# The same row numbers and own engine orders for pair 0, with the next tile's block loads issued between group 0's and group 1's row gathers

## The chip, the cores and the metric

One core of one Trainium2 chip. The metric is the device time of one execution in microseconds (us). The times of several runs are given as a median; one further execution was profiled, and all rows below come from it.

## What is computed

32 samples of 32 tokens with 256 channels run through four layers, each added to its input: windowed attention over a paged key/value cache, two mixing layers with weights picked per sample, and a gated feed-forward with low-rank adapters per sample. Cut to what matters:

```python
def reference(x, table, lens, cond, subj, side, ...):
    # attention: q, k, v from x; rms norm of q and k; rope; new k, v written into the cache
    # at positions lens + t; each query sees the 128 last positions up to its own
    x = x + attention(x, Wq, Wk, Wv, Wo, q_scale, k_scale, k_blocks, v_blocks, table, lens)
    x = x + einsum('bct,bcd->bdt', x, L1_weights[cond])
    x = x + einsum('bct,bcd->bdt', x, L2_weights[subj]) + side[subj][:, :, None]
    gate = lora_linear(x, Wg, Ag, Bg, subj)
    up = lora_linear(x, Wu, Au, Bu, subj)
    return x + lora_linear(silu(gate) * up, Wd, Ad, Bd, subj)
```

The cache lies in blocks of 16 positions; `table` names 257 blocks per sample, of which 11 can matter for a query window.

## The kernel before, in words

The kernel is written by hand, engine by engine: each engine has a fixed list of instructions, and semaphores join them.

**Units of work.** The 32 samples form 8 groups of 4 (128 tokens, one row of the partitions each), and two groups form a pair. Attention and the mixing layers go by group, the feed-forward by pair (256 tokens as the moving side of the products). The old cache is read by tiles of 8 samples, so tile t serves pair t.

**Cache rows.** For each tile GpSimd loads the blocks (`load_blocks`, L623 to L628: one indirect DMA for k, one for v, both into the buffer `early`), and SyncE stores them from `early` as rows of 256 values into a table in device memory (`scatter_rows`, L534 to L543, eight stores). The new k and v of all samples, held in `new_kv`, are stored behind them (`new_rows`, L545). Then GpSimd gathers for each group the 160 rows per sample that its queries see (`prepare`, L640 to L656: four indirect DMAs `far` and one `near`). Their row numbers (`rows`, then `place_i`) are computed on VectorE and TensorE (L991 to L1004). `prepare` of a group waits for the tile's stores, for the new rows and, from group 2 on, for the P.V products of the group two before it, whose buffer it takes. `load_blocks` of a tile waits for the stores of the tile before, since there is one `early`.

**Prologue.** Projections of v and k, then q (L1217), the rope products on VectorE, squares and roots for the norms on ScalarE (`root`, L732), turning q (L1240) and spreading its scales.

**Attention of a group**, in stages: "kt" transposes the gathered keys, "scores" multiplies, adds the mask and takes the row maxima on VectorE (L1069) and the exponentials on ScalarE (L778), "den" takes the reciprocals on VectorE (L1081) and scales the probabilities on GpSimd (`normalise`, L658 to L669), "pt0" and "pt1" transpose them, "pv" multiplies by v, "wo" projects and adds to x, "mix" applies the composed mixer, "xt" and "xf" turn the result and split it into a high and a low part for the feed-forward.

**Mixer.** The two mixing layers are composed on the chip into one matrix per sample: block matrices `first_bd` and `second_bd` are transposed ("first", L1312) and multiplied ("prod", L1320) in two halves of four groups. The buffers of these two are taken by Wd afterwards (`d_raw`), so SyncE waits for the second product (L587, semaphore `mixer_psum`) before it loads Wd.

**Feed-forward of a pair.** Each operand is split in a high and a low part and each product is three matmuls (L1427): "lora", "adapt", "gate0" to "up7", "down..", "tail..". Pair 0 has attention alone; during the feed-forward of pair m the attention of pair m + 1 is interleaved. The weights are split once, step by step, during pair 0 and the first feed-forward ("high" on ScalarE, "low" on VectorE, "split" both, L799 and L1168; TensorE waits for a split with "use").

**What sets the order.** `START_ORDER` (pair 0), `FIRST_ORDER` (feed-forward 0 with attention of pair 1) and `LOOP_ORDER` are lists of steps; every engine walks the same list and takes its part of each step. GpSimd takes only "den", "gather" and "load".

**SyncE's queue** is one list: inputs, tile 0's stores, new rows, mixer rows, adapter weights a, g0, mixer blocks, b0, u0, tile 1's stores, b1, g1, u1, then behind the wait for the mixer Wd (L589), eight loads of Ad (L594), Bd (L596), and the stores of tiles 2 and 3.

## Time and profile before

| | us |
|---|---|
| median of 3 runs | 257.56 (257.46 to 262.0) |
| profiled execution, its own time | 257.65 |
| its span | 255.2 |
| TensorE busy | 209.8 (82%) |
| VectorE busy | 142.6 (56%) |
| ScalarE busy | 105.2 (41%) |
| GpSimd busy | 76.8 (30%) |

The span is what lies between the first and the last instruction that the profiler saw; the execution's own time is 2.45 us more. TensorE's busy time is the longest, but it has idle stretches in the first half: the slices of the page show it full only from about 130 us on. PE is TensorE, DVE VectorE, ACT ScalarE, POOL GpSimd, SP SyncE; a q behind a name is its queue of DMA issues.

### The profile page before, as it was taken

To read this page: it belongs to the slowest core of one execution; us is meant where nothing else is said; L and a number is where in the kernel's file an instruction comes from. 1 tells how busy PE (TensorE), PEld (TensorE's weight loads), DVE (VectorE), ACT (ScalarE), POOL (GpSimd) and SP (SyncE) were. 2 spreads that over 40 slices of the span, in tenths; PEclk is the share of its full clock that TensorE was granted. 3 is DMA by queue.
4 is the path that set the end of the run, shared out by engine and by line. 5 is a ranking of instruction groups with operands and counts; after the bars stand their busy time and mean duration, and the time that the engine had idled before them with its cause. 6 is when DMAs were issued, how large, how long until landed. Compare 5 with 4: busy or idle time off the path is not lost.

```text
span 255.2 us, 5101 instructions
## 1 busy us (share of the span) xinstructions
PE 209.8 (82%) x1995; PEld 190.1 (75%) x1995; DVE 142.6 (56%) x486; ACT 105.2 (41%) x290; POOL 76.8 (30%) x90
## 2 busy tenths in 40 slices
PE   2696968478768649892999799999979999989995
PEld 1675858367456638882988799888878988889995
DVE  5745979575457545696514754741665454236522
ACT  2146228595532652557012733452282364213310
POOL 3520047543677040048242325045240013000000
PEclk9999999956999977998599999999999999999999
DMA  6988799669942988815795003001300000010001
GB/s 167 264 167 111 188 180 326 180 124 136 240 161 91 249 143 111 132 49 134 160 144 145 5 0 105 0 3 46 100 0 4 0 3 0 3 41 3 0 0 44
DMA packets 64124, 25.25 MB, mean 99 GB/s; under 512 B 55780, under 2 KB 60836, under 8 KB 63524
## 3 DMA queue, kind: packets, MB, share of 16 engines
q1 hardware_dynamic: 60432, 14.07, 27.5%
q0 software_dynamic: 2944, 10.23, 15.5%
q10 hardware_dynamic: 724, 0.62, 0.8%
q8 instruction: 16, 0.26, 0.5%
q14 instruction: 8, 0.07, 0.1%
HBM read 17.83 MB, written 7.08 MB: 98 GB/s over the span
## 4 chain that ended last, share of the span: by engine, by line
PE 44%; DVE 14%; issue 12%; POOL 11%; SPq 7%; ACT 6%; DMA 5%; POOLq 1%; ACTq 0%; DVEq 0%
PE bank L1427 27%; PE bank L1217 6%; POOL far L651 5%; SPq L594 4%; POOL prob L665 4%; DMA early<-in_kb,blk_i 3%; SPq L540 3%; ACT prob L778 2%; DVE prob L1069 2%; PE bank L1374 2%; PE bank L1413 2%; DVE mask L1048 1%; PE bank L1393 1%; PE bank L1206 1%; DVE low_raw L1115 1%
## 5 line engine op out<-in xcount | busy, mean ns | idle before, releaser
L651 POOL DMA_INDIRECT far<-table_rows,place_i x32 | 31.7, 991 | 63.2 <-issue 26.4
L1427 PE MATMUL bank<-xf_high,gu_high 128*128 128x256 f32 x128 | 39.0, 305 | 0.2 <-DVE b_low L1168 0.2
L778 ACT ACTIVATE prob<-prob,ntop,qscale 128x160 f32<-128x160 f32 x64 | 32.4, 508 | 15.9 <-DVE ntop L1075 15.9
L1427 PE MATMUL bank<-xf_high,gu_low 128*128 128x256 f32 x128 | 36.4, 284 | 0.0
L1427 PE MATMUL bank<-xf_low,gu_high 128*128 128x256 f32 x128 | 36.4, 284 | 0.0
L665 POOL TENSOR_TENSOR prob<-prob,rden 128x512 f32<-128x512 f32 x16 | 17.1, 1066 | 61.6 <-DVE rden L1081 61.5
L1105 DVE SCALAR_TENSOR_TENSOR gs<-th,bank 128x256 f32<-128x256 f32 x32 | 13.4, 419 | 26.5 <-ACT th L813 26.1
L1427 PEld LDWEIGHTS bank<-xf_high,gu_high 128*128 128x128 f32 x128 | 24.5, 192 | 1.7 <-issue 1.0
L1374 PE MATMUL bank<-k,prob 128*128 128x128 f32 x64 | 13.1, 340 | 14.7 <-POOL prob L665 14.7
L1427 PEld LDWEIGHTS bank<-xf_low,gu_high 128*128 128x128 f32 x128 | 24.5, 191 | 0.2
L1427 PEld LDWEIGHTS bank<-xf_high,gu_low 128*128 128x128 f32 x128 | 24.4, 191 | 0.0
L813 ACT ACTIVATE th<-bank 128x256 f32<-128x256 f32 x32 | 11.9, 379 | 27.8 <-PE bank L1427 27.8
L1374 PEld LDWEIGHTS bank<-k,prob 128*128 128x128 f32 x64 | 8.9, 171 | 17.5 <-POOL prob L665 17.4
L1427 PE MATMUL bank<-d_high,h_high 128*128 128x256 f32 x64 | 20.6, 322 | 0.0
L1069 DVE CUSTOM_DVE_ANT_0 prob<-bank,mask 128x160 f32<-128x160 f32 x64 | 17.0, 320 | 4.8 <-PE bank L1366 4.8
L1427 PE MATMUL bank<-low_high,b_high 128*128 128x256 f32 x64 | 18.7, 292 | 0.2
L1427 PE MATMUL bank<-d_low,h_high 128*128 128x256 f32 x64 | 18.7, 292 | 0.0
L1427 PE MATMUL bank<-d_high,h_low 128*128 128x256 f32 x64 | 18.5, 289 | 0.0
L1427 PE MATMUL bank<-low_low,b_high 128*128 128x256 f32 x64 | 18.2, 284 | 0.0
L1427 PE MATMUL bank<-low_high,b_low 128*128 128x256 f32 x64 | 18.2, 284 | 0.0
L1098 DVE TENSOR_TENSOR h_low<-hf,h_high 128x256 fp32r<-128x256 f32 x32 | 16.1, 504 | 0.1
L1366 PE MATMUL bank<-k_t,q_bd 64*128 64x160 f32 x128 | 12.0, 331 | 3.4 <-ACT k_t L772 1.3
(220 smaller groups left out, 527.3 us busy)
## 6 DMA issues: line engine op xcount, KB each, us to landing
table_rows<-early SPq DMA_DIRECT2D x32, 144.0 KB
table_rows<-far_probs SPq DMA_DIRECT2D x2, 512.0 KB, 3.9
gu_raw<-in_Wg SPq DMA_DIRECT2D x2, 512.0 KB, 5.5
gu_raw<-in_Wu SPq DMA_DIRECT2D x2, 512.0 KB, 6.0
d_raw<-in_Wd SPq DMA_DIRECT2D x2, 512.0 KB, 8.9
out<-xs SPq DMA_DIRECT2D x8, 128.0 KB, 1.8
xs<-in_x ACTq DMA_DIRECT2D x1, 512.0 KB, 4.9
xs<-in_x SPq DMA_DIRECT2D x1, 512.0 KB, 5.8
```

Of the source, the lines that this page charges most:

```text
L594: sp.dma_start(ad_raw[:, k * NR:(k + 1) * NR].rearrange("p (n r) -> p n r", r=RANK), Ad[:, k * P:(k + 1) * P, :].rearrange("n p r -> p n r ...
L651: pool.indirect_dma_start(far[r][:, s, :], None, seen, bass.IndirectOffsetOnAxis(ap=far_i[:, GB * n + s:GB * n + s + 1], axis=0)).then_inc ...
L665: pool.tensor_tensor(v, v, over(scale, 2, P), ALU.mult).then_inc(prob_ready, 1)
L778: last = act.activation(v, v, ACT.Exp, bias=ntop[r][:, j:j + 1], scale=qscale[:, n, j:j + 1], accum_out=den[r][:, j:j + 1])
L813: act.activation(th[f % 3][:, :], FFN_BANKS[f % 3][:, 0:PAIR_TOK], ACT.Tanh, scale=0.5).then_inc(tanh_ready, 1)
L1069: last = dve.tensor_tensor_reduce(prob[twin(n)][:, j // 2, j % 2, :], b[(2, 0)[half] + j % 2][:, s * SPAN:(s + 1) * SPAN], mask[twin(n)][: ...
L1098: dve.tensor_tensor(h_low[:, f, :], hf[f % 2][:, :], h_high[:, f, :].bitcast(F32), ALU.subtract).then_inc(h_ready, 1)
L1105: dve.scalar_tensor_tensor(gs[f % 2][:, :], th[f % 3][:, :], 1.0, b[:, 0:PAIR_TOK], ALU.add, ALU.mult).then_inc(gs_ready, 1)
L1217: last = pe.matmul(bank[dst][:, t * D:(t + 1) * D], x_t[:, k, 2 * i + t, :], w_vkq[:, k, cols], start=(k == 0), stop=(k == KD - 1))
L1366: last = pe.matmul(b[(2, 0)[half] + c][:, s * SPAN:(s + 1) * SPAN], q_bd[q, n, 2 * half + s, :, :, :].rearrange("p c h t -> p (c h t)"), k ...
L1374: last = pe.transpose(b[2 + half][:, j * P:(j + 1) * P], prob[twin(n)][:, 2 * half + j // 2, j % 2, 0:P], ident)
L1427: last = pe.matmul(dst, w[a], x[b], start=start and n == 0, stop=stop and n == 2)
```

## The change

It gives each engine a list of its own for pair 0, moves parts of the prologue, and moves one pair of block loads.

- **Row numbers**: on VectorE their computation stands before the rope products of k, on TensorE their sums stand before the second projection of v and k and their transposes before the projections of q. The broadcasts of `subj` and of the norm scales go to bank 6. The addition to the mixer's diagonal stands behind `place_i`.
- **ScalarE**: the table for the square root is loaded ahead by a primer, the first root stands before the last squares of k, w_o is copied last; on TensorE w_o's transposes stand last.
- **SyncE**: Wo is loaded behind the new rows; b1 is loaded before tile 1's stores.
- **GpSimd**: `prepare(0)`, `load_blocks(1)`, `prepare(1)`. For pair 0 it no longer scales probabilities.
- **Pair 0**: `START_PE`, `START_ACT`, `START_DVE`, `START_POOL`. New stages "exp0" and "exp1" (exponentials of one half) on ScalarE, "norm0" and "norm1" (reciprocals and scaling of one half) on VectorE.
- **First feed-forward**: "kt" of group 2 before "up0", the second half of the mixer ("first", 1 and "prod", 1) behind the scores of group 2, b1's split behind "gate0", the mask of group 2 already in pair 0. The wait for the mixer moves from the scores to the transposes.

```diff
+START_PE = [("kt", 0), ("scores", 0), ("first", 0), ("kt", 1), ("pt0", 0), ("scores", 1), ("pt1", 0), ("prod", 0),
+            ("pv", 0), ("wo", 0), ("mix", 0), ("pt0", 1), ("xt", 0), ("pt1", 1), ("pv", 1), ("wo", 1), ("mix", 1), ("xt", 1)]
...
+START_POOL = [("gather", 0), ("gather", 1), ("load", 2)]
 FIRST_ORDER = (
-    [("use", "a"), "lora", "adapt", ("low", "b1"), ("mask", 0), ("use", "g0"), "gate0", ("first", 1), ("use", "u0"), ("use", "b1"),
-     "up0",
-     ("kt", 0), ("prod", 1), ("scores", 0), ("mask", 1), "gate1", "up1", ("den", 0), "gate2",
...
+    [("use", "a"), "lora", "adapt", ("use", "g0"), "gate0", ("low", "b1"), ("use", "u0"), ("use", "b1"), ("kt", 0), "up0",
+     ("scores", 0), ("mask", 1), "gate1", ("first", 1), "up1", ("den", 0), ("prod", 1), "gate2", "up2",
...
@@ SyncE
-            for a in range(2):
-                for h in range(GS):
-                    sp.dma_start(wo_raw[:, a, h, :].rearrange("p (g d) -> p g d", g=G),
...
             new_rows(0)
             new_rows(1)
+            for a in range(2):
+                for h in range(GS):
+                    sp.dma_start(wo_raw[:, a, h, :].rearrange("p (g d) -> p g d", g=G),
...
                 if a == 0:
                     gate_up("u0", Wu, 1, lower)
-                    scatter_rows(1)
+            scatter_rows(1)
@@ GpSimd
-            for r in R:
-                prepare(r, r)
+            prepare(0, 0)
             load_blocks(1)
+            prepare(1, 1)
@@ ScalarE
+            act.activation(primer[:, 1:2], ones[:, 0:1], ACT.Sqrt)
             for i in range(4):
                 take_vk(i)
-            root(1, 0, KHALF * G)
+                if i == 2:
+                    root(1, 0, KHALF * G)
@@ VectorE
+                elif stage in ("norm0", "norm1"):
+                    half = int(stage[4])
+                    dve.wait_ge(exp_ready, 2 * n + half + 1)
+                    q = slice(4 * half, 4 * half + 4)
+                    dve.reciprocal(rden[r][:, q], den[r][:, q]).then_inc(rden_ready, 1)
...
+                    dve.tensor_tensor(v, v, over(rden[r][:, q], 2, P), ALU.mult).then_inc(prob_ready, 1)
...
@@ TensorE
                 else:
-                    pe.wait_ge(x1_ready, 1)
+                    pe.wait_ge(top_ready, 6)
```

GpSimd, from the side gather of the prologue to the first work on pair 1, before. `early` is the block buffer, `far` and `near` are a group's gathered rows, `prob` its probabilities:

```order
L637 DMA side_b<-in_side,subj_i 32x32
L651 DMA far<-table_rows,place_i 128x256 x4
L654 DMA near<-table_rows,place_i 128x256
L651 DMA far<-table_rows,place_i 128x256 x4
L654 DMA near<-table_rows,place_i 128x256
L627 DMA early<-in_kb,blk_i 72x2048
L627 DMA early<-in_vb,blk_i 72x2048
```

and in the changed kernel, with the semaphores that each waits for:

```order
L643 DMA side_b<-in_side,subj_i 32x32
L657 DMA far<-table_rows,place_i 128x256 [waits v_out0,new_out,k_out0,place_ready]
L657 DMA far<-table_rows,place_i 128x256 x3
L660 DMA near<-table_rows,place_i 128x256
L633 DMA early<-in_kb,blk_i 72x2048 [waits k_out0]
L633 DMA early<-in_vb,blk_i 72x2048 [waits v_out0]
L657 DMA far<-table_rows,place_i 128x256 [waits v_out0,new_out,k_out0,place_ready]
L657 DMA far<-table_rows,place_i 128x256 x3
L660 DMA near<-table_rows,place_i 128x256
```

The two loads into `early` have moved ahead of the five gathers of group 1.

ScalarE in pair 0, from the key copy of group 0, before. `a_high` and `gu_high` are weight splits, `mixer` is the copy of the first mixer product, `prob` rows are the exponentials, half a group each two rows:

```order
L772 COPY k_t<-bank 128x4x128 [waits kt_psum]
L778 ACTIVATE prob,den<-prob,ntop,qscale 128x160 [waits ntop_ready]
L778 ACTIVATE prob,den<-prob,ntop,qscale 128x160 x3
L778 ACTIVATE prob,den<-prob,ntop,qscale 128x160 [waits ntop_ready]
L778 ACTIVATE prob,den<-prob,ntop,qscale 128x160 x3
L799 CAST a_high<-a_raw 128x512 [waits w_in_a]
L799 CAST gu_high<-gu_raw 128x2x512 [waits w_in_g0]
L778 ACTIVATE prob,den<-prob,ntop,qscale 128x160 [waits ntop_ready]
L778 ACTIVATE prob,den<-prob,ntop,qscale 128x160 x3
L778 ACTIVATE prob,den<-prob,ntop,qscale 128x160 [waits ntop_ready]
L778 ACTIVATE prob,den<-prob,ntop,qscale 128x160 x3
L783 COPY far_probs<-bank 128x512 [waits pfar_psum]
```

and now, from group 0's second half of exponentials:

```order
L786 ACTIVATE prob,den<-prob,ntop,qscale 128x160 [waits ntop_ready]
L786 ACTIVATE prob,den<-prob,ntop,qscale 128x160 x3
L791 COPY far_probs<-bank 128x512 [waits pfar_psum]
L807 CAST a_high<-a_raw 128x512 [waits w_in_a]
L840 COPY mixer<-bank 128x512 [waits mixer_psum]
L786 ACTIVATE prob,den<-prob,ntop,qscale 128x160 [waits ntop_ready]
L786 ACTIVATE prob,den<-prob,ntop,qscale 128x160 x3
L794 COPY o_t<-bank 128x4x2x32 [waits o_psum]
L786 ACTIVATE prob,den<-prob,ntop,qscale 128x160 [waits ntop_ready]
L786 ACTIVATE prob,den<-prob,ntop,qscale 128x160 x3
```

The copies of the transposed probabilities of group 0 and of the mixer product now stand ahead of the exponentials of group 1.

TensorE in the first feed-forward, from "up0"'s last product, before. `first_bd` rows are the transposes of the mixer's second half, `second_bd` rows its product, `far` and `near` the keys and `k_t` the scores of group 2:

```order
L1427 MATMUL bank<-low_high,b_low 128x256
L1345 MATMUL bank<-k,far 128x128 [waits firstt_ready,o_ready,xf_ready,x1_ready,kv_in0]
L1345 MATMUL bank<-k,far 128x128 x3
L1346 MATMUL bank<-k,near 128x128
L1320 MATMUL bank<-second_bd,first_t 128x128 [waits x3_ready,firstt_ready]
L1320 MATMUL bank<-second_bd,first_t 128x128 x3
L1366 MATMUL bank<-k_t,q_bd 128x160 [waits mixer_ready,x3_ready,xf_ready,near_kt_ready,far_kt_ready]
L1366 MATMUL bank<-k_t,q_bd 128x160 x7
```

and now, from the scores of group 2 ("up0" stands before them, the first three products are "gate1", the nine behind the transposes, of which five rows are shown, "up1"):

```order
L1381 MATMUL bank<-k_t,q_bd 128x160 [waits x3_ready,xf_ready,near_kt_ready,far_kt_ready]
L1381 MATMUL bank<-k_t,q_bd 128x160 x7
L1444 MATMUL bank<-low_high,b_high 128x256
L1444 MATMUL bank<-low_low,b_high 128x256
L1444 MATMUL bank<-low_high,b_low 128x256
L1333 MATMUL bank<-k,first_bd 128x128 [waits top_ready]
L1333 MATMUL bank<-k,first_bd 128x128 x3
...
L1444 MATMUL bank<-low_high,b_high 128x256
L1444 MATMUL bank<-low_low,b_high 128x256
L1444 MATMUL bank<-low_high,b_low 128x256
L1339 MATMUL bank<-second_bd,first_t 128x128 [waits firstt_ready]
L1339 MATMUL bank<-second_bd,first_t 128x128 x3
```

The product of the second half stood before the scores of group 2 and now stands behind them, "gate1" and "up1", and its transposes wait for the row maxima (`top_ready`).

## Rows read from the trace of the kernel before

**Rows 1.** The chain that ended last, 82 to 125 us: start, duration, what.

```profile
82.58 0.37 SPq L589
...
84.51 4.35 SPq L594
...
94.42 15.74 issue
...
110.93 0.99 POOL far L651
...
120.18 1.07 POOL prob L665
...
121.29 1.12 PE bank L1374 x4
```

**Rows 2.** Timeline of SyncE's queue: start, duration from first to last issue, what.

```profile
82.58 0.92 SPq L589 DMA_DIRECT2D d_raw<-in_Wd  x2
83.54 13.64 SPq L594 DMA_DIRECT2D ad_raw<-in_Ad  x8
...
97.92 35.40 SPq L540 DMA_DIRECT2D table_rows<-early  x16
```

**Rows 3.** Timeline of GpSimd, first and last gather of pair 0 and the loads.

```profile
34.52 0.97 POOL L651 DMA_INDIRECT far<-table_rows,place_i  x1 [20.09 <-DVE place_i L1004]
...
45.80 0.95 POOL L654 DMA_INDIRECT near<-table_rows,place_i  x1 [0.30 <-issue]
47.05 0.97 POOL L627 DMA_INDIRECT early<-in_kb,blk_i  x1 [0.30 <-issue]
```

**Rows 4.** Store of new rows (L550, the later took 3.1) and side gather (L637), with landing.

```profile
L550 SPq DMA_DIRECT2D table_rows<-far_probs x2: 359/666/972, 26.5 to 30.1; - x2
...
DMA to landing us min/median/max: 3.1/3.9/4.7
...
L637 POOL DMA_INDIRECT side_b<-in_side,subj_i x1: 877/877/877, 13.6 to 13.6; - x1
...
DMA to landing us min/median/max: 6.9/6.9/6.9
```

**Rows 5.** The v block loads of tile 1 and tile 2 (L627), with landing.

```profile
L627 POOL DMA_INDIRECT early<-in_vb,blk_i x1: 969/969/969, 48.3 to 48.3; - x1
...
DMA to landing us min/median/max: 8.8/8.8/8.8
...
L627 POOL DMA_INDIRECT early<-in_vb,blk_i x1: 964/964/964, 82.6 to 82.6; - x1
...
DMA to landing us min/median/max: 11.1/11.1/11.1
```

**Rows 6.** Windows: stretch, length, busy per engine, PEclk, DMA share, GB/s.

```profile
39.40:44.40 5.00, 4.10 (x43) 3.82 (x42) 4.49 (x15) 4.15 (x8) 3.79 (x4) 1.00 1.08 319
47.00:50.70 3.70, 1.36 (x16) 1.12 (x16) 2.42 (x19) 1.38 (x6) 1.94 (x2) 1.00 0.66 158
86.00:90.00 4.00, 1.83 (x16) 1.62 (x14) 2.00 (x11) 4.00 (x18) 0.00 (x0) 1.00 1.09 290
```

**Rows 7.** Timeline of TensorE: keys and scores of group 1, products, transposes of group 2.

```profile
50.78 0.66 PE L1345 MATMUL bank<-k,far 128*128 128x128 f32 x4 [2.18 <-DMA near<-table_rows,place_i]
...
52.78 2.50 PE L1366 MATMUL bank<-k_t,q_bd 64*128 64x160 f32 x16 [1.23 <-DVE k_t L1057]
...
73.84 0.36 PE L1427 MATMUL bank<-xf_high,a_high 128*128 128x256 f32 x1 [1.01 <-DVE xf_low L1093]
...
78.97 0.36 PE L1427 MATMUL bank<-xf_high,gu_high 128*128 128x256 f32 x1 [0.16 <-DVE b_low L1168]
...
92.58 1.12 PE L1374 MATMUL bank<-k,prob 128*128 128x128 f32 x4 [4.76 <-POOL prob L665]
```

**Rows 8.** Timeline of VectorE: a two-input product of 512 elements, a mask.

```profile
29.33 0.69 DVE L977 TENSOR_TENSOR far_probs<-k_sin,rstd 128x512 f32<-128x512 f32 x1
...
50.61 1.26 DVE L1048 SCALAR_TENSOR_TENSOR mask<-k,thresh 128x160 f32<-128x160 f32 x4
```

124 lines of the change are left out of this document (66 added, 58 removed), and 1 row of the table FIRST_ORDER.

## The prediction

> **What bounds the kernel now.** I read the chain that ended last first. Up to 73 us it runs through the attention of pair 0. Between 82.6 and 121.3 us it is no engine at all: it leaves TensorE for SyncE's queue [rows 1]. The loads of Wd (L589) start at 82.58, when the second half of the mixer has been composed on TensorE. Behind them stand eight loads of Ad (L594), of which the second holds the queue 4.35 us and the third about as long, and only then the sixteen stores of two cache tiles. GpSimd's gather of group 4 waits for the first eight until 110.93. GpSimd's order is fixed: behind that gather come the next block loads, and the softmax scaling of group 3 only at 120.18. TensorE has been done with its second down piece since 116.66 and starts the transposes of group 3 at 121.29, 4.63 us idle.
>
> SyncE's timeline gives the three points of this path [rows 2]: Wd at 82.58, the stores of tile 2 at 97.92 (15.3 us later), the gather 13.0 us after that. From there to 121.29 are 10.4 us of GpSimd. Then the kernel is mostly products to the end. So what happens before 80 us counts only through one number: when the Wd loads may start. That is what I work out.
>
> **Part 1, the prologue.** The row numbers are made on VectorE before the k path instead of behind it: some 2.5 us of small operations, which now fill the time in which VectorE waited 2.8 us for the square root. Moving ScalarE's table load (1.28 us) ahead removes that wait. k of the second half is then ready at 29.5 instead of 30.0, and the row numbers at once behind it, 4.4 us earlier than 34.25. But the gather also waits for the store of the new rows, issued 30.1 and landing 3.1 us later, 33.2 [rows 4]. It is the next to be late: the first gather goes at 33.1 instead of 34.52 [rows 3], a gain of 1.4 us. The rotation of q on VectorE starts when the last q projection is done, 32.8 instead of 34.8; w_o's transposes now sit before the key transposes of group 0, and these come at 43.8 instead of 45.25. Group 0 gains 1.4 us.
>
> **Part 2, the block loads between the gathers.** Five gathers of group 0 take 5 x 1.255 = 6.3 us, so the loads of tile 1 go at 39.4 and 40.7 instead of 47.05 and 48.33 [rows 3], and the five gathers of group 1 from 41.95, the last at 46.95 instead of 45.80. In the old kernel that last one landed at 50.7 and TensorE took the keys of group 1 at 50.78 [rows 7]. What do the loads in front of them cost? The nearest row: at the start of the program a gather of 4 KB (L637) issued behind a pair of such loads at 13.56 took 6.9 us, until 20.5, after the second load had landed (19.1) [rows 4]. So a gather behind a load lands behind it. Lower bound: no such order, 46.95 + 3.0 = 49.9. The second load takes 8.8 us with little beside it, 40.7 + 8.8 = 49.5, and 11.1 us beside other traffic, 51.8 [rows 5]; behind it 5 x 128 KB, about 3 us at some 200 GB/s (the windows of rows 6 have 158 to 319). That is 52.5 to 55, upper bound 56. The transfers now meet the weight loads: the 16 engines are full from 33.2 to 44.4 already (share 1.08 in its second half) and at 0.66 after 47 [rows 6]; to that come Wo (0.25 MB) and the first part of Bu (0.5 MB). I take 53.7 us for the keys of group 1, 2.9 later than before.
>
> The Trainium skill, "DMA: Bandwidth & Descriptors", section "Queues, rings and completion order", says that each DMA engine consumes the descriptors of one ring in order, which speaks against this move. The row of the 4 KB gather agrees. Without that rule the keys would be there at 49.9 and the total 3.8 us less than the sum below.
>
> **Part 3, the own orders for pair 0.** TensorE places the keys of group 1 ahead of the first transposes of group 0's probabilities, ready since 52.0; so group 0 waits too. Then: group 1's scores at the lower clock 2.50 us [rows 7], transposes 1.4, mixer product 1.9. ScalarE now stands with the mixer copy in front of group 1's exponentials, so these begin at about 61, where they began at 55.65. Against it: the scaling on VectorE takes about 0.7 us per half (the nearest row is L977, two inputs of the same shape, 0.69 [rows 8]) against 1.04 on GpSimd, and it does not wait behind two weight splits. Walking the four queues piece by piece from the keys of group 1 to the first feed-forward product I get 22.5 us: keys and copies 2.2, scores 2.5, transposes and mixer product 3.3, copy and four exponentials 2.7, o_t, Wo and x1 2.0, two scalings with the mask of group 2 between them (1.26 in [rows 8]) 3.5, transposes, their copies, P.V, Wo, mixing and split 6.3. Before it was 73.84 - 50.78 = 23.1. So the feed-forward of pair 0 begins at 53.7 + 22.5 = 76.2 instead of 73.84.
>
> **Part 4, the second half of the mixer.** Before, its product ended 8.7 us after the first feed-forward product. Now it stands behind "up0", the scores of group 2, "gate1" and "up1", and its transposes wait for all maxima of group 2. From the start S of the feed-forward: the split b1 ends at S + 5.1 (78.97 - 73.84 [rows 7], unchanged), keys 0.7, up0 1.1, tanh and two VectorE operations 1.3, so maxima from S + 8.2, 2.4 us, to S + 10.6; transposes 0.5, up1 1.1 (the copy of the transposes with the mask before it, 1.2 + 0.7, ends at S + 12.5), product 1.0 and rounding: S + 13.7. Wd goes at 89.9 instead of 82.58: +7.3 us.
>
> **Part 5, what SyncE's queue gives back.** In the old kernel the loads of tile 2 (issued 81.3 and 82.6, the later one landing at 93.65) run beside Wd, and the DMA engines are full (1.09 from 86 to 90 [rows 5, 6]). Now GpSimd gathers pair 1 from about 63 (the first P.V of pair 0 releases it; tile 1's stores are done at about 61 instead of 67.7) and from about 72, and issues those loads at 78; they are down at 87. Wd is then alone: 0.5 MB loads issued back to back at 65.1 and 65.6 landed after 5.5 and 6.3 us, so the third Ad load gives the queue free at +6.5 instead of +11.1, and the stores follow at +10.8 instead of +15.3. Saving 4.5 us; bounds 0 and 7.5 (every issue at its shortest).
>
> **The sum.** Stores of tile 2: 89.9 + 10.8 = 100.7 against 97.92, +2.8 us. Stores, gather, block loads and scaling from there on keep their 23.4 us (97.92 to 121.29 [rows 1, 2]). TensorE does not take the bound back: it reaches these transposes at S + 40.7 = 116.9, counting that its 4.76 us of idle at 92.58 [rows 7] shrinks to 1.5, and waits for GpSimd until 124.1. The profiled execution was 257.65 us (span 255.2 and 2.45 around it), the median 257.56: 257.65 + 2.8 = 260.4. Bounds: keys of group 1 at 49.9 (-3.8) or 56 (+2.3); the queue's saving 7.5 (-3) or 0 (+4.5).
>
> **Rivals.**
> A, the queue is not late: the gathers of group 1 are not held, pair 0 runs partly at the full clock, and the faster drain wins. 257.65 + 2.8 - 3.8 - 1 = 255.7. For it: SyncE's queue clearly suffers from the block loads now. Against: the 4 KB gather.
> B, slower by more than 2%: TensorE stays at its lower clock. In the old kernel it fell to 1.2 GHz after the idle stretch around 50 us (kt to scores of group 1: 2.50 us for what takes 1.36 at 47.25) and came back at 62 [rows 7]. In the new one it idles some 4 us before group 1's keys and is busy only half of 62 to 76. If it goes into the feed-forward at 1.2 GHz, lora and gate0 (30 products at 0.12 us a start) cost 3 us more, and pair 0 one to two, all ahead of Wd: 260.4 + 4.5 = 264.9. It decides once the extra delay is over 2.4 us. Against: gaps of the same kind at 63 to 73 left the clock up.
> C, faster by more than 2%: GpSimd's wait goes altogether and TensorE is the bound. It reaches the transposes at S + 40.7; with S = 72 that is 112.7 against 121.3, 249 us. It needs Wd before 79 us, against Part 4.
> D, the moves hide: everything before 80 us is swallowed and Wd is as late as the queue is shorter, 257.5.
>
> **How the numbers follow.** Forecast (259 to 262.5) 0.48, A 0.18, B 0.17, D 0.14, C 0.03. The range 255 to 265 takes in A, D and most of B. 2% is 5.15 us, about what a measurement of this kernel tells from no change: faster by more 0.03, within 0.79, slower by more (over 262.8: B and the upper edge of the forecast) 0.18.
>
> **What would show it.** First gather near 33.1; block loads of tile 1 at 39.4; group 1's keys on TensorE at 52 to 55; first feed-forward product 74.5 to 78; Wd's loads 88 to 92 with the mixer product as releaser; no Ad load holding the queue for 4 us twice; tile 2's stores near 100.7; TensorE idle 6 us or more before the transposes of group 3. It is wrong if Wd starts before 86 us, if the gathers of group 1 land before 51, or if that idle time on TensorE is gone.

## The result, and the profile after

The changed kernel takes 267.54 us (median of 4 executions, 265.05 to 269.31); the kernel before, on the same chip and beside it, 258.93 (257.46 to 262.0). The ratio is 1.0359, with a 95% interval of 1.0298 to 1.042: slower by 3.6%. The profiled execution took 266.96 us, its span 265.1. The ratios and their intervals leave out executions over 1.5% above the fastest of the same kernel (1 of 4 here, 6 of 11 in f3, 5 of 10 in f2, 2 of 4 in f4, 4 of 6 in g1) while the medians take all, so a ratio can differ from the quotient of two medians.

The page of the changed kernel, TensorE's slices with the granted clock and the DMA share under them, and the chain's shares:

```profile
PE   2798886048577978893199979999998999989995
...
PEclk9999999856965879999579999999999999999999
DMA  6787999999723609791578601200400000010001
...
PE 41%; issue 12%; DVE 12%; POOL 8%; ACT 6%; DMA 4%; SPq 1%; POOLq 0%
```

A slice is 6.6 us. TensorE has a slice with nothing (46 to 53 us), and a slice of 1 at 126 to 133 us. The DMA engines are full from 27 to 66 us. "issue", 12% of the chain, is for the most part GpSimd's wait for the stores of a cache tile, in which the profile shows nothing to wait for.

GpSimd's timeline (start, duration, what, idle time before it): first and last gather of group 0, the two block loads, first and last gather of group 1, first gather of group 4, scaling of group 3. It answers to [rows 3] and to the end of [rows 1].

```profile
33.30 0.97 POOL L657 DMA_INDIRECT far<-table_rows,place_i  x1 [18.93 <-DMA table_rows<-far_probs]
...
38.34 0.95 POOL L660 DMA_INDIRECT near<-table_rows,place_i  x1 [0.30 <-issue]
39.59 0.97 POOL L633 DMA_INDIRECT early<-in_kb,blk_i  x1 [0.31 <-issue]
...
47.23 0.95 POOL L660 DMA_INDIRECT near<-table_rows,place_i  x1 [0.31 <-issue]
...
121.66 0.99 POOL L657 DMA_INDIRECT far<-table_rows,place_i  x1 [19.72 <-issue]
...
130.57 1.05 POOL L671 TENSOR_TENSOR prob<-prob,rden 128x512 f32<-128x512 f32 x1
```

TensorE's timeline: keys of group 0, first half of the mixer's blocks, keys and scores of group 1, the Wo product of group 1, the first feed-forward products, the mixer's second product, the transposes of group 3 [rows 7].

```profile
43.84 0.66 PE L1362 MATMUL bank<-k,far 128*128 128x128 f32 x4 [0.58 <-DMA near<-table_rows,place_i]
...
54.23 1.11 PE L1333 MATMUL bank<-k,first_bd 128*128 128x128 f32 x4 [7.60 <-DMA second_bd<-mix_rows]
57.69 1.12 PE L1362 MATMUL bank<-k,far 128*128 128x128 f32 x4 [2.33 <-DMA near<-table_rows,place_i]
...
60.04 2.50 PE L1381 MATMUL bank<-k_t,q_bd 64*128 64x160 f32 x16 [0.17 <-issue]
...
76.18 2.08 PE L1424 MATMUL bank<-w_o,o_t 128*128 128x256 f32 x4 [0.61 <-ACT o_t L794]
...
82.26 0.55 PE L1444 MATMUL bank<-xf_high,a_high 128*128 128x256 f32 x1 [1.01 <-DVE xf_low L1114]
...
96.42 1.91 PE L1339 MATMUL bank<-second_bd,first_t 128*128 128x128 f32 x8
...
131.68 1.11 PE L1391 MATMUL bank<-k,prob 128*128 128x128 f32 x4 [9.68 <-POOL prob L671]
```

SyncE's queue: the mixer's blocks, Bu, the stores of tile 1, and from Wd to the stores of tile 2 [rows 2].

```profile
39.76 2.07 SPq L559 DMA_DIRECT2D second_bd<-mix_rows  x4
...
43.46 0.99 SPq L587 DMA_DIRECT2D b_raw<-in_Bu  x1
48.85 15.32 SPq L541 DMA_DIRECT2D table_rows<-early  x8
...
98.36 0.92 SPq L595 DMA_DIRECT2D d_raw<-in_Wd  x2
99.32 8.37 SPq L600 DMA_DIRECT2D ad_raw<-in_Ad  x8
...
108.43 38.18 SPq L541 DMA_DIRECT2D table_rows<-early  x16
```

Read against the rows of before, the distance grows in three steps. The keys of group 1 come at 57.69 instead of 50.78: +6.9. From them to the first feed-forward product S it is 24.6 us instead of 23.1, and from S to the end of the mixer's second product, right behind which Wd is loaded, 16.1 instead of 8.7: +7.4. Then SyncE's queue gives back 5.3: Wd to the stores of tile 2 is 10.1 instead of 15.3 us. In sum the stores are 10.5 us later (108.43 against 97.92). From there all is as before: 13.2 us to the gather, 10.0 to the transposes, with TensorE idle for 9.68 instead of 4.63 us. The transposes are 10.4 us later and the span is 9.9 longer.

### The profile page after: what moved, and what is told of

Its sections match the earlier page's. It is cut to its first block, busy times and chain, and to the rows that moved or that the text cites. A ratio compares the mean times of both kernels' runs of the same rounds, so it can differ in the third digit from the quotient of the medians.

```text
span 265.1 us, 5104 instructions
## 1 busy us (share of the span) xinstructions
PE 212.7 (80%) x1995; PEld 191.6 (72%) x1995; DVE 142.8 (54%) x494; ACT 105.2 (40%) x291; POOL 70.2 (26%) x82
## 4 chain that ended last, share of the span: by engine, by line
PE 41%; issue 12%; DVE 12%; POOL 8%; ACT 6%; DMA 4%; SPq 1%; POOLq 0%
PE bank L1444 28%; DMA near<-table_rows,place_i 4%; POOL prob L671 3%; ACT prob L786 3%; DVE prob L1077 3%; POOL far L657 3%; PE bank L1391 3%; PE bank L1430 2%; PE bank L1410 1%; DVE mask L1056 1%; PE bank L1424 1%; POOL early L633 1%; DVE xs L1111 1%; PE bank L1339 1%; PE bank L1381 1%
## 5 line engine op out<-in xcount | busy, mean ns | idle before, releaser
L786 ACT ACTIVATE prob<-prob,ntop,qscale 128x160 f32<-128x160 f32 x64 | 32.4, 508 | 14.9 <-DVE ntop L1083 14.9
L671 POOL TENSOR_TENSOR prob<-prob,rden 128x512 f32<-128x512 f32 x12 | 12.5, 1042 | 56.3 <-DVE rden L1102 56.3
L1444 PEld LDWEIGHTS bank<-xf_high,gu_high 128*128 128x128 f32 x128 | 25.1, 196 | 1.3 <-issue 0.9
L1444 PEld LDWEIGHTS bank<-xf_high,gu_low 128*128 128x128 f32 x128 | 25.0, 195 | 0.0
L1391 PE MATMUL bank<-k,prob 128*128 128x128 f32 x64 | 12.2, 322 | 14.2 <-POOL prob L671 14.0
L1391 PEld LDWEIGHTS bank<-k,prob 128*128 128x128 f32 x64 | 8.2, 161 | 17.2 <-POOL prob L671 16.0
L1238 PE MATMUL bank<-w_vkq,x_t 128*128 128x256 f32 x64 | 14.6, 384 | 1.1 <-ACT w_vkq L758 1.1
L811 ACT CAST h_high<-hf 128x256 fp32r<-128x256 f32 x32 | 12.7, 398 | 4.0 <-DVE hf L1129 4.0
## 6 DMA issues: line engine op xcount, KB each, us to landing
gu_raw<-in_Wu SPq DMA_DIRECT2D x2, 512.0 KB, 10.4
```

The costliest lines, as they stand in the source:

```text
L671: pool.tensor_tensor(v, v, over(scale, 2, P), ALU.mult).then_inc(prob_ready, 1)
L786: last = act.activation(v, v, ACT.Exp, bias=ntop[r][:, j:j + 1], scale=qscale[:, n, j:j + 1], accum_out=den[r][:, j:j + 1])
L811: act.copy(h_high[:, f, :], hf[f % 2][:, :]).then_inc(hhigh_ready, 1)
L1238: last = pe.matmul(bank[dst][:, t * D:(t + 1) * D], x_t[:, k, 2 * i + t, :], w_vkq[:, k, cols], start=(k == 0), stop=(k == KD - 1))
L1391: last = pe.transpose(b[2 + half][:, j * P:(j + 1) * P], prob[twin(n)][:, 2 * half + j // 2, j % 2, 0:P], ident)
L1444: last = pe.matmul(dst, w[a], x[b], start=start and n == 0, stop=stop and n == 2)
```

## The experiments

"Keys after gather" below is the time from the first gather of group 0 to the keys of group 1 on TensorE, "S to mixer" that from the first feed-forward product to the end of the mixer's second product, each from the profiled execution. S is the start of the first feed-forward product. The low stretches are the times between 40 and 92 us in which the windows of 1 us show TensorE's granted clock at its lower level. The five kernels after, e3, f2, f3 and g3 are alike in their block loads and in SyncE's list up to tile 1's stores; their 23.3 to 24.4 us to the keys show how far this time varies from one profiled execution to the next.

| kernel | median us (executions) | keys after gather | S | S to mixer | Wd to stores | low stretches |
|---|---|---|---|---|---|---|
| before | 258.93 (4) | 16.3 | 73.8 | 8.7 | 15.3 | 51-62 |
| after | 267.54 (4) | 24.4 | 82.3 | 16.1 | 10.1 | 51-64, 74-88 |
| e1_load_behind | 262.22 (4) | 20.1 | 79.2 | 13.6 | 10.3 | 50-60, 67-74 |
| e2_load_only | 261.92 (4) | 21.0 | 81.4 | 9.9 | 12.3 | 56-67, 80-87 |
| e3_stores_wait | 263.93 (6) | 24.0 | 83.2 | 14.9 | 9.7 | 49-63, 70-87 |
| e4_ad_first | 251.73 (4) | 15.4 | 73.7 | 9.9 | 4.2 | 53-60, 73-77 |
| f1_queue_back | 264.4 (4) | 22.3 | 80.8 | 14.8 | 10.0 | 51-61, 68-85 |
| f2_ad_first_after | 256.85 (10) | 23.4 | 82.2 | 14.8 | 1.0 | 52-62, 69-86 |
| f3_mixer_early | 260.38 (11) | 23.6 | 86.8 | 9.1 | 10.4 | 53-67, 70-91 |
| f4_both_back | 261.85 (4) | 16.3 | 75.4 | 14.8 | 9.4 | 48-55, 62-79 |
| g1_best | 254.77 (6) | 15.0 | 77.7 | 9.1 | 3.0 | 51-58, 61-82 |
| g2_wo_back | 265.84 (4) | 23.7 | 80.6 | 14.9 | 9.9 | 50-61, 71-85 |
| g3_busy_wait | 264.15 (4) | 23.3 | 79.6 | 15.9 | 9.2 | 71-85 |
| g4_ad_first_busy | 251.75 (6) | 15.9 | 76.0 | 9.0 | 9.7 | 77-80 |

The kernel before ran beside each set: its medians were 259.19 (e1 to e4), 258.05 (f1 to f4), 257.25 (g1 to g3) and 257.64 (g4).

### What makes the keys of group 1 late

Two suspects: the block loads in front of group 1's gathers, and SyncE's new list, which puts Wo (0.25 MB) and Bu (0.5 MB) ahead of or beside them. e1 takes away the first, f1 the second, f4 both; e2 puts the loads alone into the kernel before.

**e1_load_behind** (the changed kernel):

```diff
-            prepare(0, 0)
+            for r in R:
+                prepare(r, r)
             load_blocks(1)
-            prepare(1, 1)
```

> The changed kernel with one thing put back: the block loads of tile 1 behind both groups' gathers. Theory L (the loads in front of the gathers make group 1 late): the keys of group 1 are on TensorE at 49 to 51 instead of 57.7, Wd starts 6 to 8 us earlier than 98.4 and the total falls to 258 to 261. Theory W (it is Wo and Bu, which SyncE now loads between 29 and 45, that fill the DMA engines): the mixer blocks still land near 54, group 1's keys come only behind them, near 54 or later, and the total stays above 263.

The last gather of group 1 went at 47.5 and its keys came 8.6 us later. Before it was 5.0 us, in the changed kernel 10.4. 262.22 us beside 259.19; three of the four executions took 261.62 to 262.86, one 257.29. Neither theory was met: the keys came at 56.1 and the total lies between the two.

**e2_load_only** (the kernel before, with the edit of e1 the other way round).

> The kernel before with only the block loads of tile 1 moved between the two groups' gathers. Theory L: group 1's keys come 5 us or more later than 50.8, Wd starts later than 82.6 by as much, the stores of tile 2 by less since the queue is free of block loads, total 259 to 264. Theory W: group 1's keys come 1 to 3 us later and the total stays within 2 us of the kernel before.

The keys came 21.0 us after the first gather instead of 16.3, and the time was 261.92 us beside 259.19, ratio 1.0111 (0.9957 to 1.0266). The loads alone cost 4.7 us at the keys, and some 1% at the end, which the interval does not tell from nothing.

**f1_queue_back** (the changed kernel): Wo's loads back to the start, Bu behind the stores of tile 1.

```diff
+            for a in range(2):
+                for h in range(GS):
+                    sp.dma_start(wo_raw[:, a, h, :].rearrange("p (g d) -> p g d", g=G),
...
             def scatter_rows(t):
...
             new_rows(1)
-            for a in range(2):
-                for h in range(GS):
-                    sp.dma_start(wo_raw[:, a, h, :].rearrange("p (g d) -> p g d", g=G),
...
                     gate_up("u0", Wu, 1, lower)
-            scatter_rows(1)
+                    scatter_rows(1)
```

> The changed kernel with SyncE's list put back (Wo at the start, Bu behind tile 1's stores); the block loads stay between the gathers. From the first gather to group 1's keys on TensorE it was 16.3 us in the kernel before, 20.0 with only the loads put back, 20.9 with only the loads moved, 24.4 in the changed kernel. If both causes add (loads in front some 4.5 us, Wo and Bu some 4), this run has 20 to 21.5 us, and the total is 261 to 264. If the loads in front are the whole cause, it has 24 and the total stays at 266.

The keys came 22.3 us after the first gather, 2.1 less than in the changed kernel and 1.1 to 2.1 less than in the five alike; 264.4 us, ratio 1.0302 (1.0209 to 1.0394).

**f4_both_back** (the edits of e1 and f1 together).

> The changed kernel with SyncE's list and the block loads both put back; the earlier row numbers, the table load ahead and the own orders stay. Both causes gone: 16 to 17 us from the first gather to group 1's keys (near 49.5 to 51), the first feed-forward product near 73, Wd near 87, the stores of tile 2 near 98, total 256 to 259, the same as the kernel before. If the own orders themselves are slow, the total is above 261 although the keys are in time.

16.3 us, as before the change. With e1 and f1 this is a square of four, from the first gather to the keys: 16.3 (neither), 20.1 (SyncE's list), 22.3 (loads between), 24.4 (both). SyncE's list alone costs 3.8 us, the loads alone 6.0, both 8.1. On top of the loads SyncE's list is worth 2.1 us in this pair. By the landing of the last gather (22.3 us behind the first in f3, 23.3 in g3, 23.4 in f2, 22.3 in f1) it may be worth nothing, so it is the lesser of the two. The loads' share has a plain part, 2.5 us of GpSimd's issues in front of group 1's gathers. The rest is landing: from the last gather to the keys 8.6 us with SyncE's list, 8.2 with the loads, 10.4 with both. With neither, the last gather landed after 3.4 us and TensorE came to the keys 1.6 us later, without a wait.

With the keys on time again f4 still took 261.85 us, ratio 1.0223 (1.0108 to 1.0339). The rival of its expectation was met: what is left of the change, pair 0's own orders and the later place of the mixer's second half, makes the kernel slower by itself. From the keys to S it is 25.5 us (49.97 to 75.44), where the kernel before has 23.1, and from S to the mixer's product 14.8 against 8.7.

The two block loads of tile 1 in the trace of the changed kernel, with their landing. The k load took 9.2 us, the v load 13.8, against 8.8 for the v load in [rows 5]:

```profile
L633 POOL DMA_INDIRECT early<-in_kb,blk_i x1: 970/970/970, 39.6 to 39.6; - x1
L633 POOL DMA_INDIRECT early<-in_vb,blk_i x1: 972/972/972, 40.9 to 40.9; - x1
...
DMA to landing us min/median/max: 9.2/11.5/13.8
```

40.9 + 13.8 = 54.7, and 3 us later group 1's keys start. The v load of f1, where SyncE's list is that of before:

```profile
L633 POOL DMA_INDIRECT early<-in_vb,blk_i x1: 1101/1101/1101, 41.3 to 41.3; - x1
...
DMA to landing us min/median/max: 13.1/13.1/13.1
```

It is hardly shorter, and in g2 (Bu early, Wo not) it took 14.4 us; e3, f2, f3 and g3 had 12.0 to 13.2. With the loads behind the gathers it took 8.2 and 8.3 us with SyncE's list of before (f4, g1) and 10.7 with the new one (e1). So most of the v load's delay comes with its place near 41 us, under either list, and not from what the change adds to the list.

In the changed kernel the mixer's blocks, in SyncE's queue, land late too: of the eight transfers of L559 the median landed after 4.4 us, the slowest after 12.9. Windows of the same trace (columns as in [rows 6]): the DMA engines are full but move only 161 to 196 GB/s from 46 to 50 us, and then 313 and 383:

```profile
46.00:48.00 2.00, 0.63 (x10) 0.39 (x6) 1.72 (x14) 0.46 (x2) 1.69 (x2) 1.00 1.07 161
48.00:50.00 2.00, 0.00 (x0) 0.00 (x0) 1.87 (x11) 2.00 (x10) 0.18 (x1) 1.00 1.08 196
...
52.00:54.00 2.00, 0.00 (x0) 0.00 (x0) 0.00 (x0) 0.00 (x0) 0.00 (x0) 0.50 1.01 313
54.00:56.00 2.00, 1.11 (x4) 0.71 (x4) 0.61 (x2) 0.00 (x0) 0.00 (x0) 0.50 1.04 383
```

The Trainium skill, "DMA: Bandwidth & Descriptors", section "Issuing engines are not separate DMA queues", says that transfers started by different engines run on the same 16 DMA engines and interleave. The square agrees: SyncE's list alone lengthened the time from GpSimd's last gather to its landing from 3.4 us (f4) to 8.6 (e1).

**e3_stores_wait** (the changed kernel): a third suspect, the stores of tile 1, which start at 48.85 beside group 1's gathers.

```diff
+            sp.wait_ge(kv_in[1], 16 * (GB + 1))
             scatter_rows(1)
```

> The changed kernel, where SyncE waits until group 1's rows have landed before it stores tile 1. If the stores that start at 48.85 compete with these gathers (theory S), the gathers land near 53 instead of 57.6, and the total falls by 2 to 4 us. If only the loads in front and the weights hold them (theory L or W), the gathers land within 1 us of before, the stores start 9 us later, and the total is the same or more, since the gathers of pair 1 then start at about 70 to 75.

The keys came 24.0 us after the first gather instead of 24.4. SyncE's timeline has the stores 8 us later than in the changed kernel:

```profile
56.81 8.54 SPq L541 DMA_DIRECT2D table_rows<-early  x8
```

These stores wait for group 1's rows, so the rows had landed by 56.8, at most 8.8 us behind the last gather. Other kernels with the stores beside the gathers have 8.3 (f3), 9.4 (f2, g3) and 10.4 (changed), and theory S wanted the rows near 53: it isn't the stores. TensorE took the keys later still, because its list has the transposes of the mixer's blocks in front of them, and these waited for the blocks until 57.15 (in f3 until 58.52):

```profile
57.15 1.11 PE L1334 MATMUL bank<-k,first_bd 128*128 128x128 f32 x4 [9.56 <-DMA second_bd<-mix_rows]
58.06 1.06 PE L1363 MATMUL bank<-k,far 128*128 128x128 f32 x4
```

The time was 263.93 us, ratio 1.0161 (1.0054 to 1.0269), better than the changed kernel's by more than the keys explain; why stays open. Its executions had a higher granted clock (0.939 in the middle, 0.923 in the changed kernel's); whether that is the cause isn't shown.

**g2_wo_back** splits SyncE's list: only Wo's loads go back to the start, Bu stays.

> The changed kernel with only Wo's four loads put back to the start of SyncE's list; Bu stays ahead of tile 1's stores and the block loads stay between the gathers. It splits what SyncE's list costs group 1's keys (24.4 us behind the first gather in the changed kernel, 22.2 with both put back). If Wo at 29.5 us is what is in the way (it stands ahead of the mixer's round trip and beside the gathers): the keys 22 to 22.5 us behind the first gather, the mixer's rows back by 50 instead of 54, 264.5 to 266. If it is Bu (0.5 MB more at 43.5): 24 to 24.5 us, the mixer's rows as late as before or little earlier, 266.5 to 268.

The keys came 23.7 us after the gather, the mixer's transposes at 48.5 instead of 54.2, and 265.84 us, ratio 1.0352 (1.0299 to 1.0405). So with the loads in front it takes Wo at 29.5 us to hold the mixer's rows; in e1, with Wo there and the loads behind, TensorE did not wait for them either. What Wo and Bu each cost the keys isn't shown: 23.7 us lies within the 23.3 to 24.4 of the five alike. With the mixer's transposes 5.8 us earlier the total is the same within its interval: that wait of 7.60 us lay beside the longer one for the keys.

### What lies between the keys and Wd

**f3_mixer_early** (the changed kernel with the first feed-forward order of before, less the mask that pair 0 now makes, and with the waits that belong to it, which the lines below leave out): the mixer's second half ahead of group 2's scores.

```diff
 FIRST_ORDER = (
-    [("use", "a"), "lora", "adapt", ("use", "g0"), "gate0", ("low", "b1"), ...
-     ("scores", 0), ("mask", 1), "gate1", ("first", 1), "up1", ("den", 0), ("prod", 1), "gate2", "up2",
+    [("use", "a"), "lora", "adapt", ("low", "b1"), ("use", "g0"), "gate0", ("first", 1), ("use", "u0"), ("use", "b1"),
+     "up0",
+     ("kt", 0), ("prod", 1), ("scores", 0), ("mask", 1), "gate1", "up1", ("den", 0), "gate2",
```

> The changed kernel with the first feed-forward's list of before: the second half of the mixer is composed ahead of the scores of group 2. From the first feed-forward product to the end of the mixer product it is 9 to 10 us instead of 16.0, so Wd and the stores of tile 2 come about 5 to 6 us earlier, and the total falls by 4 to 6 us, to 261 to 263. The rival, that this list only moves an idle time of TensorE and SyncE's queue is bound by its transfers, has the stores of tile 2 less than 2 us earlier and the total above 264.

S to mixer fell from 16.1 to 9.1 us, and the time to 260.38 beside 258.05, ratio 1.0027 (0.996 to 1.0094), and 0.9% slower by the medians. So it is level with the kernel before or nearly, though the keys are as late as ever (23.6). Of what was put back one by one this took away most of the loss (the ratio fell from 1.036 to 1.003; with both causes of the late keys put back, in f4, to 1.022).

**f2_ad_first_after** and **e4_ad_first** ask whether SyncE's queue is the path. In both, Ad and Bd are loaded ahead of Wd and of its wait for the mixer; f2 is the changed kernel, e4 the kernel before.

```diff
+            sp.wait_ge(ssum_ready, SUMS)
+            for k in range(NF):
+                sp.dma_start(ad_raw[:, k * NR:(k + 1) * NR].rearrange("p (n r) -> p n r", r=RANK),
...
+            sp.dma_start(bd_raw[:, :], Bd.rearrange("n r f -> (n r) f")).then_inc(w_in["bd"], 16)
             sp.wait_ge(mixer_psum, 2)
...
-            sp.wait_ge(ssum_ready, SUMS)
-            for k in range(NF):
...
-            sp.dma_start(bd_raw[:, :], Bd.rearrange("n r f -> (n r) f")).then_inc(w_in["bd"], 16)
```

> The kernel before with the eight Ad loads and Bd in SyncE's list ahead of the wait for the mixer and of Wd. If SyncE's queue from Wd to the stores of tile 2 sets the end, as the prediction has it, the stores of tile 2 start when the v blocks have landed, near 93.5, at the latest, instead of 97.9, TensorE's idle time before the transposes of group 3 falls from 4.6 us to about 0 to 1, and the total is 252 to 255. If something else bounds (a rival: TensorE and the exponentials), the total stays at 257 to 258.

> The changed kernel with the Ad and Bd loads ahead of SyncE's wait for the mixer. If the late mixer costs time only through SyncE's queue, the stores of tile 2 start within 2 us of Wd (near 100 instead of 108.4), the gather of group 4 comes near 112 to 114, TensorE's idle time before the transposes of group 3 falls from 9.7 us to below 3, and the total is 257 to 260. If pair 0's lateness itself sets the end (TensorE), the total stays above 263.

e4: 251.73 us, ratio 0.9784 (0.9668 to 0.99), faster than before. f2: 256.85 us, ratio 0.9885 (0.9821 to 0.9949), so one edit takes some 4% off the changed kernel (267.54 to 256.85). Part of that goes with the clock, which was 0.923 in the middle of the changed kernel's executions and 0.947 in f2's: at 0.934 and 0.935 the two took 258.97 to 260.87 and 265.05, some 5 us apart. The keys of group 1 are late in f2 (23.4) and its mixer product too (97.1), yet they no longer reach the end in full: the stores of tile 2 go 1.0 us after Wd and TensorE waits 1.06 us ahead of the transposes of group 3. In e4 it does not wait at all. SyncE's queue of e4, then its transposes of group 3 on TensorE, which have no idle time before them:

```profile
65.76 10.07 SPq L589 DMA_DIRECT2D ad_raw<-in_Ad  x8
75.87 0.83 SPq L591 DMA_DIRECT2D bd_raw<-in_Bd  x1
83.69 1.54 SPq L594 DMA_DIRECT2D d_raw<-in_Wd  x2
87.88 41.51 SPq L540 DMA_DIRECT2D table_rows<-early  x16
```

```profile
116.54 0.66 PE L1374 MATMUL bank<-k,prob 128*128 128x128 f32 x4
```

The eight Ad loads still take 10 us of the queue, but from 65.76 on, and are over at 75.8, before the mixer's product lets Wd go at 83.7. The stores follow at 87.88 instead of 97.92, the transposes stand at 116.54 instead of 121.29.

### The clock

Every kernel with pair 0's own orders shows a stretch at the lower clock somewhere in 61 to 91 us (last column of the table), in most of them 14 to 21 us long and reaching into the feed-forward; the kernel before, e2, e4 and g4, with the old order, show 0 to 7 us there. It does not hang on late keys: f4 has them as early as before, and is low from 62 to 79. Nor does it take a long wait: in the 6 us before that fall TensorE's longest idle time was 1.20 us. Windows of f4 from 62 to 80 us (columns as in [rows 6]):

```profile
62.00:68.00 6.00, 4.50 (x46) 3.15 (x44) 4.57 (x12) 3.11 (x5) 1.25 (x2) 0.50 0.94 215
68.00:74.00 6.00, 4.09 (x43) 2.22 (x40) 2.21 (x4) 1.79 (x3) 4.93 (x4) 0.50 0.55 186
74.00:80.00 6.00, 4.99 (x27) 4.62 (x27) 2.49 (x5) 1.94 (x3) 4.68 (x4) 0.58 0.30 87
```

The same windows of the kernel before:

```profile
62.00:68.00 6.00, 4.23 (x121) 3.05 (x114) 3.63 (x5) 2.37 (x4) 4.02 (x5) 1.00 0.93 187
68.00:74.00 6.00, 2.80 (x12) 1.50 (x12) 3.45 (x5) 3.20 (x6) 4.78 (x5) 1.00 0.72 234
74.00:80.00 6.00, 5.78 (x45) 5.35 (x45) 3.76 (x9) 0.81 (x2) 4.54 (x5) 1.00 0.32 98
```

The kernel before is the less busy one from 68 to 74 (2.80 of 6 us) and keeps the clock. Which gap loses it in the new order isn't settled.

What it costs is read from e1 and the changed kernel, which have the same orders on TensorE, VectorE and ScalarE. e1's clock is back at 74, before its feed-forward, and its first products start 0.12 us apart; those of the changed kernel 0.21. TensorE's timeline of e1:

```profile
79.66 0.28 PE L1444 MATMUL bank<-xf_high,a_high 128*128 128x256 f32 x1
79.78 0.27 PE L1444 MATMUL bank<-xf_low,a_high 128*128 128x256 f32 x1
```

And of the changed kernel:

```profile
83.04 0.41 PE L1444 MATMUL bank<-xf_high,a_high 128*128 128x256 f32 x1
83.25 0.41 PE L1444 MATMUL bank<-xf_low,a_high 128*128 128x256 f32 x1
```

S to mixer is 13.6 us in e1 and 16.1 in the changed kernel. Not all of the 2.5 us is this stretch. The changed kernel falls a third time, from 95 to 98 us, while it multiplies "up1" and the mixer's product:

```profile
95.00:98.00 3.00, 3.00 (x17) 3.00 (x16) 1.52 (x4) 2.88 (x12) 0.00 (x0) 0.50 0.00 0
```

Up to the keys of group 2 (88.86) the difference to e1 is 1.5 us, behind them 0.9. The kernels with the same orders and a low clock at S but none at the mixer's product (e3, f1, f2, f4, g2) have 14.8 to 14.9 us; g3, which falls at 91 to 95, has 15.9. So the low clock at S costs 1.2 to 1.5 us, the third fall 0.9 to 1.2.

**g3_busy_wait** keeps TensorE busy in the two waits of the changed kernel that stand ahead of group 1:

```diff
+                    pe.wait_ge(top_ready, 2)
+                    for i in range(44):
+                        pe.transpose(bank[1][:, 0:P], ident, ident)
                     pe.wait_ge(mix_back, 2 * GB * 16)
-                    pe.wait_ge(top_ready, 2)
...
+                    if first and r == 1:
+                        pe.wait_ge(qt_ready, 3)
+                        for i in range(16):
+                            pe.transpose(b[0][:, 0:P], ident, ident)
                     pe.wait_ge(kv_in[r], (pair + 1) * (GB + 1) * 16)
```

> The changed kernel with 44 transposes of the identity on TensorE in its wait for the mixer's rows (47 to 54 us) and 16 more in its wait for group 1's keys, into PSUM banks that are free there. Nothing in the result uses them. They keep TensorE busy where it stood idle for 7.6 and 2.3 us. Theory (part of pair 0's lateness is the lower clock that follows this idle time): clock 1.0 from 48 to 62, group 1's scores 1.4 instead of 2.5 us, first feed-forward product 2 to 3 us earlier (80 behind a gather at 33.3), 264 to 265.5. Rival 1 (the clock falls anyway in the half busy stretch from 73 to 80, and the DMAs and the other engines set the pace): first product at most 1 us earlier, 266.5 to 268. Rival 2 (the extra work itself is late for its release): the transposes of the mixer's rows later than 54.5 and the time over 268.

The clock stayed up until 71. TensorE's timeline shows the added transposes (L1330) and the scores of group 1, 1.36 us instead of 2.50:

```profile
48.50 5.02 PE L1330 MATMUL bank<-k 128*128 128x128 f32 x44 [1.95 <-DVE top L1077]
...
58.94 1.36 PE L1387 MATMUL bank<-k_t,q_bd 64*128 64x160 f32 x16 [0.59 <-DVE k_t L1065]
```

From the keys to S it was 22.4 us instead of 24.6. The time was 264.15 us (260.6 to 265.79) beside 257.25, a quotient of 1.027. The fall at 71 to 85 came as in the others, with 15.9 us from S to mixer. So the first low stretch costs about 2 us ahead of S, and work that nothing needs kept it away; the second was not touched. That the 2 us reach the end isn't shown: the four executions lie between 260.6 and 265.79, the changed kernel's between 265.05 and 269.31, measured at another time.

### Versions that should beat both

**g1_best**: the changed kernel with the edits of f4, f3 and f2 together. What remains of the change is the early row numbers and pair 0's own orders.

> The changed kernel with four edits taken together: SyncE's list as before (Wo at the start, Bu behind tile 1's stores), the block loads of tile 1 behind all ten gathers again, the second half of the mixer ahead of group 2's scores again, and Ad and Bd loaded ahead of Wd. What stays of the change is the row numbers made first and pair 0's own engine orders. Theory (the terms I found are separate, the queue is the only pin behind 85 us, and own orders neither help nor hurt): first gather near 33.7, group 1's keys near 50, first feed-forward product 74 to 76, mixer product 9 to 10 later, tile 2's stores near 88, no wait of TensorE before the transposes of group 3; 250 to 253 us, level with the kernel before plus Ad first (251.7). If the 1.4 us of the earlier first gather reach the end: 249 to 250.5. Rival (pair 0's own orders cost the clock and this reaches the end): first product at 77 or later, 254 to 257.

254.77 us beside 257.25, ratio 0.979 (0.9716 to 0.9865). By the medians it is 0.990. The ratio is e4's (0.9784), the median is 3 us above e4's, with a granted clock of 0.936 in the middle of its executions against 0.965 in e4's. The rival's figures were met (S at 77.7, 254.77 us). One execution at a clock of 0.966 took 250.21 us. So what is left of the change did not show a gain over e4; that the lower clock alone eats what its orders save is suggested by that one execution and not shown.

**g4_ad_first_busy**: e4 with 12 transposes of the identity before the keys of group 1 and 6 before its scores.

> The kernel before with Ad and Bd loaded ahead of Wd, and with TensorE kept busy in two of its waits for group 1 (12 transposes of the identity before its keys, 6 before its scores), into PSUM banks that are free there. It is the version that I expect to be fastest. Theory (the clock that falls after the idle time around 50 us costs pair 0 some 1.5 to 2 us, and with the queue's pin gone TensorE carries them to the end): clock 1.0 from 44 to 62, group 1's scores 1.4 instead of 2.5 us, first feed-forward product 72 to 73, 249.5 to 251 us, a ratio of 0.970 to 0.976 to the kernel before, against 0.978 without the extra work. Rival (other engines set pair 0's pace, the lower clock only fills their waits): group 1's scores shorter, but the first feed-forward product at 73.5 or later and the time 251.5 to 252.5.

251.75 us (251.49 to 253.95), ratio 0.9762 (0.9704 to 0.9821), level with e4 (251.73). The scores of group 1 took 1.36 us, and the keys to S 21.4 us instead of 23.1. The profiled execution began its gathers at 38.7, 3.5 us later than e4's, with a low clock at 29 to 33 us, and took 253.95, so it says little of the others. The rival holds: the 1.7 us did not reach the end, though the clock was up from 33 to 77 us. The fastest kernels of the study are e4 and g4, 2.2 to 2.4% ahead of the kernel before; the place of the Ad loads is all that the two have in common, and e4 has nothing else.

## Why the prediction was wrong

It said 260.4 us, within 2% of before with 0.79; it was slower by 3.6%, above the range. The path was right. Three terms of the sum on it were too small, all in one direction: the keys of group 1 (4.0 us), the stage from them to S (2.1) and the one from S to Wd (2.4), less 0.7 by which the queue gave back more than foreseen. That is 7.7 us but for rounding, the whole difference between the predicted shift of tile 2's stores (+2.8) and the measured one (+10.5).

**Part 1, right.** First gather at 33.1 predicted, 33.30 measured, released by the store of the new rows as foreseen; keys of group 0 at 43.8 and 43.84. Other kernels with this prologue had the first gather at 33.3 to 36.1, so 0.2 us is partly luck.

**Part 2 failed.** Issues were right (loads 39.4 and 39.59, last gather 46.95 and 47.23). "I take 53.7 us for the keys of group 1", upper bound 56: they came at 57.69. What failed is the size of the v load: I took 8.8 to 11.1 us from [rows 5], and it took 13.8 (54.7 instead of 49.5 to 51.8). The 3 us from there to the keys were right. The two rows it came from have the load at 48 and at 82 us, and I moved it to 41, where the DMA engines are full by my own reading of [rows 6]. Its place is what cost: with SyncE's list put back (f1) it took 13.1 us, and the keys were still 6.0 us later than with neither. Wo and Bu (all of Bu, not a first part; the 0.5 MB are right), which I named and gave no price, add 3.8 us without the loads and at most 2.1 on top of them. "A gather behind a load lands behind it" holds for the last gather only: in e2 the first gather of group 1 was down at 55.4 and the v load in front of it at 57.0, in g3 at 53.0 and 54.3. The 4 KB row did not show this rule by itself either, since two gathers of the mixer's weights (L635) stood between it and the loads, the later of them down at 20.3. I had also taken the mixer's blocks at nothing; they waited until 54.23, which by g2 was hidden behind the keys here, but in e3 and f3 they held the keys.

**Part 3, too small by 2.1 us.** 22.5 us from the keys to S predicted, 24.6 measured. I had the lower clock in it for the scores of group 1 alone. It held from 51 to 64, and from 74 on again. With the first stretch gone (g3) the stage took 22.4, so that stretch is worth 2.1 us; what the second is worth ahead of S wasn't measured, and that g3 meets my 22.5 is partly luck, since the scores took 1.36 us there and not the 2.50 of my sum. On time or not, the own orders did not pay: with keys at 49.97 (f4) the stage took 25.5 us, against 23.1 before.

**Part 4, mechanism right, size too small by 2.4 us.** I had S + 13.7; e1, with the clock up from S to the mixer's product, has 13.6. The changed kernel had 16.1, with the lower clock at S and again at 95 to 98. The order itself costs 5 us (13.6 against 8.7), as predicted, and f3 shows that it matters more than the gathers for the end.

**Part 5, right.** Wd to stores 10.8 predicted, 10.07 measured, the longest Ad load holding the queue 2.5 us instead of 4.7. The block loads of tile 2 went at 84 and 86 instead of 78 and were down at 93.5, still ahead of Wd; gather 13.0 and 13.2 us behind; transposes 10.4 and 10.0 behind that. TensorE idle "6 us or more": 9.68. e4 and f2 show that this is the path by taking it away.

**The rivals.** B came true, at a chance of 0.17: the clock went into the feed-forward at its lower level, and its price of 4.5 us is what Parts 3 and 4 were short of (2.1 + 2.4). The keys' 4.0 us came on top. That the two 4.5 agree is partly luck: 0.9 to 1.2 us of the measured 4.5 belong to a third fall, which B did not have. I had tied the fall to late keys ("decides once the extra delay is over 2.4 us"). f4 refutes that condition: keys on time, clock low from 62 to 79. A is refuted by f1 and e2, where the last gather behind the loads was down after 8.2 and 6.9 us instead of 4.9. C needed Wd before 79 us and D a hidden delay; Wd went at 98.36. The range failed because B and the upper bound of Part 2 were treated as alternatives. Added up they give 260.4 + 2.3 + 4.5 = 267.2, beside 267.54.

## What to carry to other kernels

Price a transfer by what else runs at its new place, not by what it took at its old one: the v load took 8.8 us at 48 us and 12.0 to 14.4 at 41 to 43. When two moves load the same DMA engines in the same 15 us, price them together. A queue that issues stores for a later stage should not stand behind loads that block it for 10 us: look at what its blocking loads wait for, and put ahead those that wait for nothing late. After giving an engine an order of its own, read the granted clock of the stretch that follows: in nine of ten kernels with pair 0's own orders a low stretch reached into the feed-forward. And add the rivals up before setting a range, unless one excludes the other.

## What was unexpected of the hardware

- A small transfer wasn't spared when the queues were full: the slowest of the mixer's blocks landed 12.9 us after its issue beside a median of 4.4, and the keys of group 1 came 10.4 us behind the last gather instead of 5.0, while the DMA engines moved only 161 to 196 GB/s at a share of 1.07 to 1.08 (46 to 50 us).
- The same kernel takes different clocks in different executions and its time follows. f2_ad_first_after ran from 252.77 us at a mean granted clock of 0.966 to 260.87 at 0.934, 8 us apart; the kernel before from 255.65 at 0.966 to 259.74 at 0.94 in one set. The Trainium skill, "TensorE: Matmul & The Clock Gate", section "Part 1: The HAM clock gate (the "warmup" mystery)", says that the clock of the array has two levels, set by how busy it has been, and that the point where it changes varies from execution to execution. The two levels and the variation agree with these rows. The under 1% of a typical kernel that the page gives is for the ramp at the start; the 3% here lie between executions whose clock falls several times, and that the clock alone makes them isn't shown.
- Transposes of the identity in a wait kept the clock up at no cost that the trace shows: 44 of them ran from 48.50 to 53.5 us (ends are modelled), and the mixer's transposes behind them started at 53.36, in the changed kernel at 54.23.
- The clock can be lost without a long wait, and kept with less work: f4 fell at 62 us with 5.5 of the 8 us before busy and no idle time over 1.20 us, the kernel before kept it from 62 to 74 with 7.0 of 12 us busy. Which gap or mix decides isn't shown.
